# The up projection of a ternary feed-forward layer: plain fp32 products replaced by float32r passes and a stacked low-rank pass, and the next group's rows turned inside it

## The reference, cut to what matters

```python
def _bitlinear(x, w_latent):
    scale = clip(mean(abs(w_latent), axis=1, keepdims=True), 1e-05, None)
    tern = clip(round(w_latent / scale), -1.0, 1.0)      # -1, 0 or 1
    return x @ (tern * scale).T
...
h = _bitlinear(x, w_fc) + gate * (x @ v.T @ fast_b.T @ u.T)   # w_fc 1024x256, v 16x256, fast_b 16x16, u 1024x16
r = jnp.maximum(h, 0.0)
return _bitlinear(r * r, w_proj)                              # w_proj 256x1024
...
x = x + _L0_ffn_ref(_layernorm(x), ...)
```

## Time and profile before

| what | us |
|---|---|
| time, median of 3 runs (3769.82 to 3777.52) | 3776.26 |
| time of the profiled execution | 3778.32 |
| its span, first to last instruction | 3776.6 |
| PE busy, share of the span | 84% |
| DVE, ACT, POOL busy | 65%, 43%, 43% |
| `ffn1` on PE: first turn to the start of the last two `down` | 1082.03 to 1254.55 |
| `ffn2` on PE: the same | 2188.12 to 2360.30 |

### The profile page before, as it was taken

How to read it: one execution, slowest core, us unless ns; L and a number is a source line. 1 busy time by engine, 2 the same in 40 slices (tenths; PEclk the granted TensorE clock), 3 DMA queues, 4 the chain that set the end, 5 groups by cost and what they waited for, 6 DMA issues and landing times. The chain is left out here.

```text
span 3776.6 us, 54058 instructions
## 1 busy us (share of the span) xinstructions
PE 3189.8 (84%) x15480; PEld 1790.7 (47%) x15481; DVE 2470.0 (65%) x4785; ACT 1640.7 (43%) x3271; POOL 1628.3 (43%) x1677
## 2 busy tenths in 40 slices
PE   7888898889789789797988999786896787998975
PEld 3333333333246543444344356554574475665564
DVE  6999899898954475684857644697245774223435
ACT  4756666666434256365454634112132232223122
POOL 4898889888844321213122145211653100001553
PEclk9999999999999889799897999997998998998997
DMA  4555455555510000000000000810243794000246
GB/s 133 143 135 137 128 137 138 127 137 139 140 29 0 16 2 2 1 2 2 2 2 1 2 1 1 224 35 1 101 145 120 187 130 59 17 11 0 73 130 210
DMA packets 357983, 283.04 MB, mean 75 GB/s; under 512 B 214026, under 2 KB 273982, under 8 KB 357728
## 3 DMA queue, kind: packets, MB, share of 16 engines
q1 hardware_dynamic: 344672, 246.43, 26.5%
q0 software_dynamic: 13056, 33.65, 2.6%
HBM read 205.69 MB, written 76.16 MB: 75 GB/s over the span
## 5 line engine op out<-in xcount | busy, mean ns | idle before, releaser
L678 POOL TENSOR_TENSOR mamba_dBu<-mamba_du,mamba_bcs 128x512 f32<-128x512 f32 x512 | 640.6, 1273 | 125.6 <-DMA mamba_bcs<-mamba_bc 80.9
L601 PE MATMUL mamba_banks<-mamba_hc,ident 128*128 128x512 f32 x1024 | 539.2, 636 | 142.6 <-DVE mamba_hc L918 142.5
L848 ACT ACTIVATE mamba_banks<-mamba_delta,mamba_a_neg 128x512 f32<-128x512 f32 x512 | 352.3, 690 | 182.5 <-DVE mamba_hc L918 170.4
L1621 DVE TENSOR_REDUCE attn_mp<-attn_banks 128x1 f32<-128x512 f32 (+3 forms) x768 | 383.9, 551 | 69.3 <-PE attn_banks L1329 48.5
L601 PEld LDWEIGHTS mamba_banks<-mamba_hc,ident 128*128 128x128 f32 x1024 | 181.9, 196 | 457.7 <-DVE mamba_hc L918 342.2
L918 DVE TENSOR_TENSOR mamba_hc<-mamba_banks,mamba_bcs 128x512 f32<-128x512 f32 x512 | 344.1, 673 | 11.4 <-PE mamba_banks L601 11.4
L911 DVE TENSOR_TENSOR_SCAN mamba_banks<-mamba_banks,mamba_dBu 128x512 f32<-128x512 f32 x256 | 312.2, 1219 | 55.8 <-ACT mamba_banks L848 36.5
L911 DVE TENSOR_TENSOR_SCAN mamba_banks<-mamba_banks,mamba_h_end,mamba_dBu 128x512 f32<-128x512 f32 x256 | 327.2, 1278 | 21.0 <-ACT mamba_banks L848 12.2
L1326 PE MATMUL attn_banks<-attn_kT,attn_qT 96*128 96x512 bf16 (+3 forms) x768 | 272.3, 374 | 12.2 <-ACT attn_kT L1510 5.0
L1341 PE MATMUL attn_banks<-attn_qT,attn_kT 98*128 98x512 bf16 (+3 forms) x768 | 247.3, 341 | 12.3 <-ACT attn_r L1529 4.8
L1013 PE MATMUL ffn_hp<-ffn_xT,ffn_w1T 128*128 128x512 f32 x512 | 230.5, 606 | 10.4 <-ACT ffn_xT L229 6.7
(11 more groups left out here) (397 smaller groups left out, 6561.8 us busy)
## 6 DMA issues: line engine op xcount, KB each, us to landing
mamba_bcs<-mamba_bc SPq DMA_DIRECT2D x256, 512.0 KB, 4.9
moe_slots_moe<-moe_pad SPq DMA_DIRECT2D x2, 9252.0 KB, 55.9
moe_xg<-moe_slots_moe SPq DMA_DIRECT2D x144, 128.5 KB, 2.1
mix_qkv<-mixA_qkv SPq DMA_DIRECT2D x8, 1536.0 KB, 5.9
mixA_y<-moe_rows SPq DMA_DIRECT2D x16, 512.0 KB, 6.0
mix_qk<-mix_qkv SPq DMA_DIRECT2D x16, 512.0 KB, 7.5
mix_v<-mix_qkv SPq DMA_DIRECT2D x16, 256.0 KB, 7.4
mix_out<-mixB_oh SPq DMA_DIRECT2D x16, 256.0 KB, 7.0
```

The source lines that it names most:

```text
L601: pe.matmul(banks[:, SUMS + k % PAIR, :], c.ident[:, :], hc[:, n % RING, :], start=False, stop=True, skip_group_check=True).then_inc(sem(" ...
L678: pool.tensor_tensor(dBu[:, n % RING, :], du[:, v, k, :], bcs[:, i_of(n) % 4, 0, :], ALU.mult)\
L848: act.activation(banks[:, n % RING, :], delta[:, v, k, :], ACT.Exp, scale=a_neg[:, k, st:st + 1])\
L1621: dve.tensor_reduce(mp[:, qt // GT, j, qt % GT, at // 512:at // 512 + 1], banks[:, item % SLOTS, 0:size], AX.X, ALU.max).then_inc(sem("rin ...
```

## The change

In the feed-forward stage `up` no longer multiplies fp32 by fp32. `w1r` holds the bare ternary values (-1, 0, 1) as float32r. The turned rows are split into a float32r part and what it leaves out (`xs`, two parts `a`, two copies `v`). Each of the two k halves is multiplied with both parts: four float32r passes for a block. The low-rank term becomes a fifth pass: `low(g)` forms `x @ v.T` once for a group in four passes (the 16 rows repeated 8 times over 128 partitions in `vst`), ACT rounds it into `ls`, DVE replaces its upper 64 partitions by the remainder, and `ust` holds `u @ fast_b * gate` divided by the scale, as a float32r part and a remainder. The scale of `w_fc` is applied as ACT's relu scale `s2` (the square of the scale, since `hp` is multiplied with the relu).

The order moves too: the next group's rows are turned after block 3 of `up`, ACT copies them after relu 5 and cast 4, DVE forms their remainder after square 5; `low(g+1)` stands inside `down`, ahead of its last quarter; DVE's moments, adds and normalising stand after the squares, two groups ahead.

```diff
     def ternary(self, dve):
         dve.wait_ge(self.work_free, 1)
         dve.memset(self.ones[:, :], 1.0).then_inc(self.diag_ready, 1)
+        dve.wait_ge(self.uf_ready, 1)
+        dve.tensor_copy(self.us, self.banks[:, 4, 0:HB * RANK].rearrange("p (b r) -> p b r", r=RANK)).then_inc(self.uf_copied, 1)
         dve.wait_ge(self.loaded, 64)
-        dve.tensor_scalar(self.ufT, self.banks[0:RANK, 4:6, :].rearrange("p a n -> p (a n)"), self.gate[:, 0:1], None,
-                          ALU.mult).then_inc(self.uf_scaled, 1)
...
+        self.low_parts(dve)
...
     def low_rank(self, pe):
-        for n in range(2):
-            mm = pe.matmul(self.banks[0:RANK, 4 + n, :], self.fb[:, :], self.uT[:, n * 512:(n + 1) * 512], start=True, stop=True)
+        for b in range(HB):
+            mm = pe.matmul(self.banks[:, 4, b * RANK:(b + 1) * RANK], self.uT[:, b * P:(b + 1) * P], self.fb[:, :], start=True, stop=True)
...
     def up(self, pe, i, bank):
         for b in range(4):
-            pe.matmul(self.banks[:, bank, b * P:(b + 1) * P], self.wfc[:, 4 * n + b, k * P:(k + 1) * P], self.c.ident[:, :],
-                      start=(b == 0), stop=False, skip_group_check=True)
-        pe.matmul(self.banks[:, bank, :], self.v[:, k * P:(k + 1) * P], self.ufT[:, n * 512:(n + 1) * 512],
-                  start=False, stop=True, skip_group_check=True).then_inc(self.tr_ready, 1)
+            mm = pe.transpose(self.banks[:, bank, b * P:(b + 1) * P], self.wfc[:, 4 * n + b, k * P:(k + 1) * P], self.c.ident[:, :])
+        mm.then_inc(self.tr_ready, 1)
...
-                pe.wait_ge(ffn.tr_used, 10)
+                pe.wait_ge(ffn.tr_used, 6)
+                ffn.low_up(pe, 0, SUMS + 1)
+                pe.wait_ge(ffn.tr_used, 7)
+                ffn.low_up(pe, 1, SUMS)
+                pe.wait_ge(ffn.tr_used, 12)
                 group_loop(pe, group)
...
+                            ffn.copy_low(act, 0, SUMS + 1)
+                            ffn.copy_low(act, 1, SUMS)
...
+                def turn(g):
+                    pe.wait_ge(norm.xn_ready, g * GT + GT)
+                    pe.wait_ge(ls_ready, g)
...
+                def low(g, v):
+                    pe.wait_ge(xlo_ready, g * KD + KD)
+                    for k in range(KD):
+                        for a in range(SP_):
+                            mm = pe.matmul(trp[:, 0, :], vst[:, k, :], xs[:, v, a, k, :], start=(k == 0 and a == 0),
+                                           stop=(k == KD - 1 and a == SP_ - 1))
+                    mm.then_inc(v_filled, 1)
+                def up(g, v, between=None):
                     for b in range(HB):
                         if not (isinstance(g, int) and g == 0 and b < 4):
                             pe.wait_ge(h_ready, g * HB + b - 3)
                         for k in range(KD):
-                            mm = pe.matmul(hp[:, b % 4, :], w1T[:, k, b * P:(b + 1) * P], norm.xT[:, k, :],
-                                           start=(k == 0), stop=(k == KD - 1))
-                        mm.then_inc(h_filled, 1)
+                            for a in range(SP_):
+                                pe.matmul(hp[:, b % 4, :], w1r[:, k, b * P:(b + 1) * P], xs[:, v, a, k, :],
+                                          start=(k == 0 and a == 0), stop=False)
+                        if b == 0:
+                            pe.wait_ge(ls_ready, g + 1)
+                        pe.matmul(hp[:, b % 4, :], ust[:, b * P:(b + 1) * P], ls[:, :], start=False, stop=True).then_inc(h_filled, 1)
+                        if b == HB // 2 - 1 and between is not None:
+                            between()
...
                 with pe.Fori(1, G // 2 - 1) as m:
-                    norm.transposes(pe, m * 2 + 1)
-                    down(m * 2 - 1, 1)
-                    up(m * 2 + 1)
+                    down(m * 2 - 1, 1, lambda: low(m * 2 + 1, 1))
+                    up(m * 2 + 1, 1, lambda: turn(m * 2 + 2))
...
+                def group(g, v, after=True):
+                    square(g, lambda: x_low(g + 1, 1 - v))
+                    if after:
+                        norm.moments(dve, g + 2)
+                    add(g - 1, 0)
+                    if after:
+                        norm.normalise(dve, g + 2)
+                    low_low(g + 1)
+                    add(g - 1, 1)
```

More of the change, by code:

```diff
@@ L357, in matrix @@
             k = first + i
[L358 to L359 removed]
+            dve.tensor_scalar(ups[i], w, self.half[:, k:k + 1], None, ALU.is_gt).then_inc(self.step, 1)
             dve.wait_ge(self.step, done + 1)
[L361 removed]
+            dve.tensor_scalar(w, w, self.nhalf[:, k:k + 1], None, ALU.is_lt).then_inc(self.step, 1)
             dve.wait_ge(self.step, done + 2)
@@ L1089, in split, with turned_rows, low, square @@
                             act.copy(hs[:, v, b - 1, 0, :], h[:, (b - 1) % HR, :]).then_inc(hi_ready, 1)
-                        if b == HB and not (isinstance(g, int) and g == G - 1):
-                            norm.copy_out(act, g + 1, h_filled, g * HB + HB)
-                norm.copy_out(act, 0)
-                def group(g, v):
-                    split(g, v)
-                pairs(act, group)
+                        if b == HB // 2 + 1 and not (isinstance(g, int) and g == G - 1):
+                            turned_rows(g + 1, 1 - v)
+                    if not (isinstance(g, int) and g == G - 1):
+                        low(g + 1)
+                def turned_rows(g, v):
+                    act.wait_ge(norm.xn_used, g + 1)
+                    for k in range(KD):
+                        act.copy(xs[:, v, 0, k, :], trp[:, k, :]).then_inc(norm.xT_ready, 1)
+                def low(g):
+                    act.wait_ge(v_filled, g + 1)
+                    act.copy(ls[:, :], trp[:, 0, :]).then_inc(ls_hi, 1)
+                turned_rows(0, 0)
+                act.copy(w1r[:, 0, :], w1b[:, 0, :]).then_inc(w1r_ready, 1)
+                low(0)
+                split(0, 0)
+                split(1, 1)
+                with act.Fori(1, G // 2 - 1) as m:
+                    split(m * 2, 0)
+                    split(m * 2 + 1, 1)
+                split(G - 2, 0)
+                split(G - 1, 1)
             @block.vector
             def _(dve):
-                def square(g):
+                def square(g, turned=None):
                     for b in range(HB):
@@ L1140, in _, with x_low @@
-                norm.moments(dve, G - 1)
-                norm.normalise(dve, G - 1)
-                square(G - 2)
-                add(G - 3)
-                square(G - 1)
-                add(G - 2)
-                add(G - 1)
+                        if b == HB // 2 + 1 and turned is not None:
+                            turned()
+                def x_low(g, v):
+                    for k in range(KD):
+                        dve.wait_ge(norm.xT_ready, g * KD + k + 1)
+                        dve.tensor_tensor(xs[:, v, 1, k, :], trp[:, k, :], xs[:, v, 0, k, :], ALU.subtract).then_inc(xlo_ready, 1)
@@ new lines, in _ @@
+                norm.moments(dve, 1)
+                low_low(0)
+                norm.normalise(dve, 1)
+                square(0, lambda: x_low(1, 1))
+                norm.moments(dve, 2)
+                low_low(1)
+                norm.normalise(dve, 2)
+                group(1, 1)
+                with dve.Fori(1, G // 2 - 1) as m:
+                    group(m * 2, 0)
+                    group(m * 2 + 1, 1)
+                group(G - 2, 0, after=False)
+                square(G - 1)
+                for g in (G - 2, G - 1):
+                    for i in range(2):
+                        add(g, i)
```

162 lines of the change are left out of this document (96 added, 66 removed).

## The result

The changed kernel takes 3718.5 us (median of four runs, 3717.0 to 3724.5) where the kernel before takes 3775.6 on the same chip: ratio 0.985, 95% interval 0.984 to 0.987. Forecast were 3713 us, range 3702 to 3732. Its profiled execution has a span of 3715.3 us, 61.3 less than that of before. By PE's first turn and its last two `down` in either stage, the 61.3 are 30.2 in `ffn1`, 29.6 in `ffn2`, 2.1 ahead of `ffn1` and 1.5 behind `ffn2`, less 2.1 between the two. The first turn of `ffn1` stands anywhere from 1077.6 to 1082.4 in the fourteen traces, so the 2.1 ahead of it are no more than traces differ by.

The account below looks back on a forecast made before the run. PE was taken to set the period of the feed-forward stages. Two stages saving 64.4 us, less 1.1 before the Mamba loop, give 63.3: 3776.3 to 3713 us, range 3702 to 3732.

Parts of the forecast that it names:

- What bounds: In the feed-forward stages PE sets the period of a group: 22.90 us, PE busy 22.55 of them.
- Price of a pass: In `up`, a float32r pass over 512 columns was put at 0.218 us, with 0.242 kept for the range.
- turn and `down`: In each steady group these PE parts stay as they were, 0.8 and 7.75 us.
- the six periods: Steady groups between a stage's first `down` and last two: 108.1 us against 135.9, saving 27.8 a stage.
- the near end: For a pass in `up`, 0.218 us, half an fp32 record, chosen over 0.242, twice a 256-column product in `down`.
- The other engines and the chain to `ls`: In a steady group, DVE, ACT and POOL stay covered under 18.15 us; `ls` is ready with 1.0 us slack.
- The start: First turn to first `down` of a stage falls from 36.6 to 32.4 us, saving 4.2.
- three waits: At a stage's start PE waits for `low_low(0)` at block 0's fifth pass, 1.1 us before `low(1)`, 2.4 for `low_low(1)`.
- the term of 2.5 us for half clock: At a stage's start, 5 us of dense work at clock 0.50 lose 2.5 us, as before.
- The rival of a lower clock: Chance 0.08: half clock lasts longer at a stage's start, up to 17.4 us more a stage, or some 5 (3723).
- The Mamba entry: Before the Mamba loop, two more ACT copies of 512 columns make PE enter later, costing 1.1 us.
- its terms 4.2 and 27.8: Savings a stage in us: 4.2 from the start-up, 27.8 from the six periods; the stage was put at about 32.2.

Follow-up runs that it names:

- halves: The changed kernel with each 512-column pass of `up` split into two products of 256 columns, `low` unsplit; ratio 0.987 to the kernel before.
- the kernel with the turn behind `up`: The changed kernel with the next group's rows turned after block 7 of `up`, not block 3, copies and remainders moved too; ratio 0.986 to the kernel before.
- the filler: The changed kernel with eight more 512-column PE products, results thrown away, behind the first turn of a stage; ratio 0.984 to the kernel before.
- bfloat16: The changed kernel with the remainder of the turned rows kept as bfloat16 and multiplied by bfloat16 weights; ratio 0.984 to the kernel before.
- three more products: The changed kernel with three more DVE products ahead of `low_low` in every group whose rows are followed by more; ratio 0.987 to the kernel before.
- one more product: The changed kernel with one more DVE product ahead of `low_low` in every group whose rows are followed by more; ratio 0.983 to the kernel before.

## Why the forecast was right, and where not

**What bounds.** Right: PE sets the period in both kernels, and taking out 12 passes shortens it by 12 passes in `ffn1`, by some 11 in `ffn2`.

**Price of a pass: the mis-sized term.** The forecast took half an fp32 record, 0.218, and kept 0.242. It is 0.233, 0.015 more; over the 44 passes of a group 0.67. A group came to 18.71 instead of 18.15 (turn and `down` took 0.1 less than their terms), the six periods to 111.4 instead of 108.1, 6.5 us in the two stages. My reason for the near end, a fixed part that weighs half as much in 512 columns, was poor: halves show it to be 0.007 an instruction. At half clock a pass takes 0.425 to 0.44 us (in the kernel with the turn behind `up`, four from 1102.32 to 1104.02, five to 1104.52), so twice the clock alone would give 0.213 to 0.22, an estimate. Why it takes 0.233 stays open; neither the type nor the length of the weight load is the cause.

**The other engines and the chain to `ls`.** Right in kind: 13.2, 10.9 and 11.7 us for DVE, ACT and POOL, and a slack of 0.75 where 1.0 was counted. One and three added products confirm it.

**The start.** 32.4 forecast, 31.0 and 31.2 measured. Two of its three waits were found, 1.5 and 2.1 for 1.1 and 2.4. The third, for `ls` in the first group, did not come: the fifth pass follows at 1086.31 (PE's timeline) without a wait, since the passes ahead of it run at half clock meanwhile. With the filler, at 1.00, it came, 1.05 us. So the term of 2.5 us for half clock was no separate cost: at full clock the same start takes 31.0, because DVE's order ends last there. That is so in this kernel only. In the kernel before with the turn moved, `ffn2` began at half clock and took 2.8 us longer to its first `down` than `ffn1` at 1.00.

The rival of a lower clock did not come in the two traces of this kernel, and in that there is luck. With waits no longer than 1.5 and 2.3 us, half clock came back in `ffn1` of three other kernels (halves, bfloat16, three more products), and the start took 32.8 us there; with one more product it did not. The windows of the same four us, with three more products, then in the changed kernel:

```profile
1104.00:1108.00 4.00, 4.00 (x12) 3.04 (x12) 2.81 (x6) 2.51 (x4) 1.51 (x2) 0.59 0.00 0
...
1104.00:1108.00 4.00, 4.00 (x23) 3.40 (x22) 2.74 (x5) 3.17 (x6) 2.47 (x2) 1.00 0.00 0
```

It came in both stages where a start-up wait grew to 4.15 and 4.00 us. With that, the rule of the Trainium skill's clock gate (TensorE: Matmul & The Clock Gate, Part 1), that an idle spell restores the throttle, agrees with the trace: the clock is at 0.50 right behind the wait of 4.15 us (the window of that kernel above), and falls to it 1 us behind the one of 4.00.

**The turn.** The forecast put no price on its place. In the kernel before it is worth 2.6 us at a stage's start at like clock (`ffn2`) and 0.4 a period, in the changed kernel 2.0 to 3.4 at the start, half clock included, and nothing later. So a part of the gain that the forecast gives to cheaper passes is the turn's.

**The Mamba entry.** Forecast: 1.1 us later. PE entered 2.15 later (70.13 for 67.98 in the earlier trace rows), yet reached `mamba_win` at 73.67, before 73.73. The ten profiled executions that turn `ust` there entered at 69.7 to 70.6 at full clock and needed 3.54 us; of the four that don't, three entered at 68.0 to 68.7 in part at half clock and needed 5.75 to 6.0, one needed 3.54. So the 2 us were paid back by the clock; that the added turns bring it up is only argued.

**Sum.** 63.3 forecast, 61.3 in the trace. Too much: 6.9 for the six periods (6.5 by the new ones, the rest because `ffn2` had 135.6 before), and 0.4 because 32.2 a stage is 0.2 more than its terms 4.2 and 27.8. Too little: 2.6 for the starts, 1.1 for an entry that cost nothing, and 1.5 by which the rest of the trace is shorter (all rounded). So the near hit of the total is in part luck: passes 7% too cheap against a start and a rest priced too dear.

## What to carry to other kernels

Price a matmul by a row of the same width class, start to start: at 128 columns a floor of 0.112 us stood under each; at 512 a shorter type bought nothing, and a split into halves cost 0.007 us for each added instruction. Where PE fills a steady loop, a pass taken out comes back whole or nearly so there, but not at the loop's start, where the order of the slowest helper engine decides and the saved passes turn into waits. A stretch at half clock costs only if nothing else ends later: look at what PE would wait for next. And a spell of half clock seen in one trace, or missing from it, need not be the kernel's own: compare several.

## What the runs showed of the hardware

With products of 128 columns PE stayed at PEclk 0.50 from 1084 to 1120 us although it was busy in all of it (the window 1100 to 1110 above); the start took 62.6 us in `ffn1`, 69.2 in `ffn2`. Being busy on the page is no guarantee of full clock.

bfloat16 weight loads, 18 of the 44 in `up` and `low`, took 2.8 us less of PEld in a group, at the same period.

A wait of 0.94 us of PE cost its group 1.24 us, 0.3 more than the idle time before the instruction shows; 0.17 of it is the overlap of the records.

Whether the clock fell behind waits of 1.3 to 2.3 us at a stage's start differed from trace to trace (PEclk 0.59 and 1.00 in the windows above) and was worth 1.8 us of a start.
